# An attention loop where VectorE weighs two value rows, GpSimd two, and TensorE adds the last two sums while it transposes

## What is computed

```
x = x + xattn(layernorm(x), ctx_1024, itok)
x = x + ffn(layernorm(x))

xattn: q = x @ Wq.T ; k, v = split(ctx @ Wkv.T) ; 16 heads of 32
  each row looks at its index and the three before it: 4 keys and 4 values
  probs = softmax(mask(q . k * 32**-0.5))        # over these 4
  out = sum over the 4 of probs * v ; out @ Wo.T
ffn: quantised gate and up (512 to 1536), sigmoid, product, down (1536 to 512)
```

## Time and profile before

| what | us |
|---|---|
| median of 3 runs | 2347.9 |
| the runs | 2347.78 to 2349.55 |
| span of the profiled execution | 2347.3 |

### The profile page before, as it was taken

The page is one execution under the profiler, slowest core; times in us unless marked ns, Lnnn a source line. Parts: engine busy times, 40 slices in busy tenths (PEclk is TensorE's granted clock), DMA queues, the critical chain, the costliest instruction groups (busy, mean ns, idle before and its releaser), DMA issues.

```text
span 2347.3 us, 25386 instructions
## 1 busy us (share of the span) xinstructions
PE 2020.4 (86%) x9524; PEld 945.0 (40%) x9524; DVE 1715.7 (73%) x1387; ACT 1398.2 (60%) x1599; POOL 670.6 (29%) x662
## 2 busy tenths in 40 slices
PE   5888888888599999999999999999000699999998
PEld 2444444444244444444444444444000344444443
DVE  8799999999634534532499998999899644577641
ACT  4678887887422322322499996676899633366530
POOL 2599999998300000000121110222111000000000
PEclk9999999999799999999999999999555899999999
DMA  7789999998346656743699995787998755555541
GB/s 297 283 314 337 348 337 346 335 350 316 126 181 226 225 207 223 259 148 144 242 378 390 378 369 209 264 320 293 401 419 327 291 229 208 205 201 232 233 152 72
DMA packets 131162, 634.60 MB, mean 270 GB/s; under 512 B 12256, under 2 KB 12768, under 8 KB 91104
## 3 DMA queue, kind: packets, MB, share of 16 engines
q1 hardware_dynamic: 85888, 316.81, 37.0%
q0 software_dynamic: 45152, 316.16, 34.6%
HBM read 430.69 MB, written 202.24 MB: 270 GB/s over the span
## 4 chain that ended last, share of the span: by engine, by line
PE 64%; issue 3%; DVE 3%; ACT 2%; POOL 0%; DVEq 0%; ACTq 0%; POOLq 0%
PE fd_pp L1777 42%; PE fd_pp L1791 21%; ACT ff_ring L1720 1%; DVE ff_sig L1575 1%; DVE ff_h_parts L1559 1%; DVE ff_sq L1497 1%; ACT ff_sig L1707 0%; DVE ff_sq L1566 0%; DVE kept_gate L1568 0%; DVE ff_gin L1510 0%; DVE ff_hq L1549 0%; ACT ff_hq L1632 0%; ACT ff_ring L1746 0%; ACT ff_sig L1736 0%; DVE kept_o_peak L1575 0%
## 5 line engine op out<-in xcount | busy, mean ns | idle before, releaser
L1791 PE MATMUL fd_pp<-ff_down,kept_gate 128*128 128x512 f16 x1536 | 458.9, 381 | 193.1 <-DVE ff_up L1616 193.1
L1777 PE MATMUL fd_pp<-ff_h_parts,kept_gate 128*128 128x512 f16 x2304 | 499.6, 380 | 14.3 <-DVE ff_h_parts L1415 14.3
L1777 PE MATMUL fd_pp<-ff_h_parts,ff_up 128*128 128x512 f16 x2304 | 497.4, 379 | 0.0
L1639 ACT ACTIVATE ff_raw<-fd_pp 128x1024 f32<-128x1024 f32 x192 | 194.3, 1017 | 396.5 <-PE fd_pp L1777 396.5
L1777 PEld LDWEIGHTS fd_pp<-ff_h_parts,kept_gate 128*128 128x128 f16 x2304 | 225.9, 98 | 287.9 <-DVE ff_h_parts L1415 14.7
L1777 PEld LDWEIGHTS fd_pp<-ff_h_parts,ff_up 128*128 128x128 f16 x2304 | 225.4, 98 | 271.8
L1420 DVE TENSOR_REDUCE kept_gate_peak<-ff_raw 128x1 f32<-128x2048 f32 x48 | 109.7, 2285 | 292.9 <-ACT ff_raw L1639 292.9
L1791 PEld LDWEIGHTS fd_pp<-ff_down,kept_gate 128*128 128x128 f16 x1536 | 150.6, 98 | 375.9 <-issue 195.8
L1791 PE MATMUL fd_pp<-ff_down,ff_up 128*128 128x512 f16 x768 | 292.2, 380 | 0.0
L1746 ACT ACTIVATE ff_ring<-ff_hq,kept_g 128x2048 int16<-128x2048 f32 x48 | 96.0, 1999 | 191.1 <-DVE ff_hq L1549 189.7
L790 PE MATMUL at_psO<-kept_wo,at_ahi 128*128 128x512 f16 x512 | 155.5, 386 | 36.2 <-ACT at_alo L277 31.6
(11 more groups left out here) (239 smaller groups left out, 3454.9 us busy)
## 6 DMA issues: line engine op xcount, KB each, us to landing
ff_raw<-up_scratch SPq DMA_DIRECT2D x66, 1024.0 KB, 8.5
gate_scratch<-ff_raw POOLq DMA_DIRECT2D x48, 1024.0 KB, 9.1
ff_gin<-gate_scratch SPq DMA_DIRECT2D x48, 1024.0 KB, 8.7
up_scratch<-ff_raw POOLq DMA_DIRECT2D x48, 1024.0 KB, 7.7
ff_gin<-gate_integers SPq DMA_DIRECT2D x73, 512.0 KB, 5.8
gate_integers<-ff_ring POOLq DMA_DIRECT2D x43, 512.0 KB, 8.7
ff_up<-up_scratch SPq DMA_DIRECT2D x21, 1024.0 KB, 9.5
kept_xs<-in_x SPq DMA_DIRECT2D x32, 512.0 KB, 14.6
```

Of the source, the lines that this page charges most:

```text
L1639: nc.scalar.activation(raw[:, n % UNITS, h * 2 * BLK:(h + 1) * 2 * BLK], pp[(2 * n + h) % 4][:, :, :].rearrange("p a t -> p (a t)"), ACT.C ...
L1777: mm = nc.tensor.matmul(pp[k % 4][:, h, :], wt[w][:, c, f:f + P], a[:, b % 2, :, c, :], start=(q == 0), stop=(q == len(todo) - 1))
L1791: mm = nc.tensor.matmul(pp[k % 8 // 2][:, k % 2, :], a[b % 2][:, f, t * P:(t + 1) * P], wt[w][:, f, :], start=(q == 0 and i == 0), stop=(q ...
```

## The change

VectorE weighs value rows 0 and 1 only. GpSimd weighs rows 2 and 3 in one instruction (`weigh_upper`), adds them to rows 0 and 1 as before, and does no second addition. `att` is gone; a tile of the same size that nobody uses keeps the other addresses. TensorE's `turn_a` waits for `half` in place of `att`, transposes row 0 into `psA` as before, and then row 1 into the same bank with four more transposes that add to what is there.

A slot of the ring is now read by TensorE to the end, so the gather into it waits for `aT`. Its place on GpSimd changes too: the gather behind tile 2s-3 stands ahead of the additions of pair `s_`, the one behind 2s-2 stays behind them. In the last pair `sum_last` has only its first addition. SP's two loads for the next section wait for `aT` in place of `att`.

```diff
--- before.py
+++ after.py
@@ -158,7 +158,8 @@
 
         xn = r.sb("xn", [P, 2, D], F32)
         xhi, xlo = (r.sb(n, [P, 2, DC, P], F16) for n in ("xhi", "xlo"))
-        att, hn = (r.sb(n, [P, 2, D], F32) for n in ("att", "hn"))
+        r.sb("gap", [P, 2, D], F32)
+        hn = r.sb("hn", [P, 2, D], F32)
         hT = r.sb("hT", [P, 4, D], F32)
         ahi, alo = (r.sb(n, [P, 2, DC, P], F16) for n in ("ahi", "alo"))
         kv = r.sb("kv_rows", [P, KR, W, 2 * D], F32)
@@ -185,7 +186,7 @@
         x1_out = [r.sem(f"x1_out{i}") for i in range(XR)]
         hT_out = [r.sem(f"hT_out{i}") for i in range(2)]
         rows_in = [r.sem(f"rows_in{i}") for i in range(KR)]
-        m = r.sems("xn xT xhi xrest xlo q prod raw sc top ds ex tot inv pr pv last half att aT ahi arest alo o x1 "
+        m = r.sems("xn xT xhi xrest xlo q prod raw sc top ds ex tot inv pr pv last half aT ahi arest alo o x1 "
                    "nmean ssq ssq_v stat aggr sqe root rstd norm x_nmean x_ssq hn hT hT_sb peak h_red h_all reduced")
 
         def blocks(t, h):
@@ -232,7 +233,7 @@
                         sp.dma_start(x1_v[p], xs[:, ring(p), :]).then_inc(x1_out[p % XR], 16)
                     p = s_ - 5
                     if p == NP - 6:
-                        sp.wait_ge(m["att"], KR * (NT // KR) - KR + 6 if NT % KR == 0 else NT - NT % KR)
+                        sp.wait_ge(m["aT"], NT - NT % KR)
                         for b in range(2):
                             sp.wait_ge(hT_out[0], 16 * (b + 1))
                             sp.wait_ge(hT_out[1], 16 * (b + 1))
@@ -521,8 +522,8 @@
                                             AX.X, ALU.add).then_inc(m["raw"], 1)
 
                 def weigh(t):
-                    values = kv[:, t % KR, 0:W - 1, D:2 * D].rearrange("p w (h e) -> p w h e", h=H)
-                    nc.vector.tensor_tensor(values, values, pr[:, t % 2, 0:W - 1].unsqueeze(3).to_broadcast([P, W - 1, H, HD]),
+                    values = kv[:, t % KR, 0:2, D:2 * D].rearrange("p w (h e) -> p w h e", h=H)
+                    nc.vector.tensor_tensor(values, values, pr[:, t % 2, 0:2].unsqueeze(3).to_broadcast([P, 2, H, HD]),
                                             ALU.mult).then_inc(m["pv"], 1)
 
                 def residual(t):
@@ -542,10 +543,6 @@
                     dve.wait_ge(m["pv"], t + 1)
                     nc.vector.tensor_tensor(kv[:, t % KR, 0:2, D:2 * D], kv[:, t % KR, 0:2, D:2 * D], kv[:, t % KR, 2:4, D:2 * D],
                                             ALU.add).then_inc(m["half"], 1)
-                    dve.wait_ge(m["half"], t + 1)
-                    dve.wait_ge(m["aT"], t - 1)
-                    nc.vector.tensor_tensor(att[:, t % 2, :], kv[:, t % KR, 0, D:2 * D], kv[:, t % KR, 1, D:2 * D],
-                                            ALU.add).then_inc(m["att"], 1)
 
                 def last_moments(t):
                     p, k = t // 2, t - (LAST - 3)
@@ -681,28 +678,25 @@
                                                 in_offset=bass.IndirectOffsetOnAxis(ap=keep["rows"][:, t:t + 1], axis=0),
                                                 element_offset=0).then_inc(rows_in[t % KR], 16)
 
-                def weigh_fourth(t):
-                    last = kv[:, t % KR, W - 1, D:2 * D].rearrange("p (h e) -> p h e", h=H)
+                def weigh_upper(t):
+                    upper = kv[:, t % KR, 2:4, D:2 * D].rearrange("p w (h e) -> p w h e", h=H)
                     pool.wait_ge(rows_in[t % KR], 16 * (t // KR + 1))
                     pool.wait_ge(m["pr"], t // 2 + 1)
                     if t < LAST - 1:
                         pool.wait_ge(m["pv"], t // 2 * 2 + 2)
-                    nc.gpsimd.tensor_tensor(last, last, pr[:, t % 2, W - 1].unsqueeze(2).to_broadcast([P, H, HD]),
+                    nc.gpsimd.tensor_tensor(upper, upper, pr[:, t % 2, 2:4].unsqueeze(3).to_broadcast([P, 2, H, HD]),
                                             ALU.mult).then_inc(m["last"], 1)
 
                 def add_up(t):
-                    weigh_fourth(t)
+                    weigh_upper(t)
                     lower, upper = kv[:, t % KR, 0:2, D:2 * D], kv[:, t % KR, 2:4, D:2 * D]
                     pool.wait_ge(m["last"], t + 1)
                     nc.gpsimd.tensor_tensor(lower, lower, upper, ALU.add).then_inc(m["half"], 1)
-                    pool.wait_ge(m["half"], t + 1)
-                    need(pool, m["aT"], t - 1)
-                    nc.gpsimd.tensor_tensor(att[:, t % 2, :], kv[:, t % KR, 0, D:2 * D], kv[:, t % KR, 1, D:2 * D],
-                                            ALU.add).then_inc(m["att"], 1)
 
                 def gather_next(t):
-                    pool.wait_ge(m["att"], t + 1)
-                    gather(t + KR)
+                    if t + KR < NT:
+                        pool.wait_ge(m["aT"], t + 1)
+                        gather(t + KR)
 
                 for t in range(KR):
                     if t == 0:
@@ -720,13 +714,14 @@
                     gather(t)
                 for s_ in range(NP + 6):
                     if s_ == NP:
-                        weigh_fourth(LAST - 1)
-                        weigh_fourth(LAST)
+                        weigh_upper(LAST - 1)
+                        weigh_upper(LAST)
                     if pair(s_ - 1) and s_ < NP:
+                        if tile(2 * s_ - 3):
+                            gather_next(2 * s_ - 3)
                         add_up(2 * s_ - 2)
                         add_up(2 * s_ - 1)
                         gather_next(2 * s_ - 2)
-                        gather_next(2 * s_ - 1)
                     if s_ > 0 and (pair(s_ - 3) or pair(s_ + 3)):
                         norms(s_)
                 nc.gpsimd.partition_all_reduce(last_all[:, :], eps_d[:, 0:1], P, PEAK).then_inc(m["reduced"], 1)
@@ -818,9 +813,13 @@
                     project(psQ[t % 2], xhi, xlo, wq, t % 2).then_inc(m["q"], 1)
 
                 def turn_a(t):
-                    pe.wait_ge(m["att"], t + 1)
+                    pe.wait_ge(m["half"], t + 1)
                     need(pe, m["alo"], t)
-                    turn(psA, att[:, t % 2, :]).then_inc(m["aT"], 1)
+                    turn(psA, kv[:, t % KR, 0, D:2 * D])
+                    for c in range(DC):
+                        mm = nc.tensor.matmul(psA[:, c, :], kv[:, t % KR, 1, D + c * P:D + (c + 1) * P], ident[:, :], is_transpose=True,
+                                              start=False, stop=(c == DC - 1), skip_group_check=True)
+                    mm.then_inc(m["aT"], 1)
 
                 def rest_a(t):
                     pe.wait_ge(m["ahi"], t + 1)
```

## The result

| | before | after |
|---|---|---|
| median | 2347.84 us | 2375.09 us |
| runs | 2346.82 to 2349.55 (4) | 2374.15 to 2375.44 (4) |
| span of the profiled execution | 2347.3 us | 2373.3 us |

The changed kernel takes 1.0117 times as long, with a 95% interval of 1.0102 to 1.0131. The forecast was 2370.4 us with a range from 2344 to 2380, so it was right in its sign and 4.7 us too low.

The account below looks back on a forecast made before the run. VectorE's back-to-back program was taken to set the 16.95 us pair. 26 pairs at +0.81 (+21.1) and ends of +1.4 gave +22.5 us on the 2347.3 us span, 0.6 under the median: 2370.4 us, range 2344 to 2380.

Parts of the forecast that it names:

- VectorE's and GpSimd's own work: Attention loop, per pair: VectorE's program falls from 16.95 to 15.90 us, GpSimd's tensor work from 9.67 to 8.70 us.
- Rival D: GpSimd's product of 1024 elements costs 2.37 us like an addition: period 17.97 us, 2376 us in all; chance 0.08.
- The wait at the queue's head: GpSimd's odd-tile gather, first in its stage, waits for TensorE's transposes until 1.75 us into each pair; products start at 3.08.
- The eight transposes: TensorE, per tile: eight transposes of `a` take 1.04 us instead of 0.60 for four, 0.44 us more.
- the 6.85 us of the forecast: From the end of VectorE's differences to the end of the odd tile's eight transposes, not shortened by VectorE's shorter weighing.
- The port: VectorE's mask and scale instruction waits for GpSimd's second addition and ends at 11.93 instead of 10.07 us: delay 1.86 us.
- Rival B: Faster: the port costs little; period 15.90 to 16.68 us, middle 16.3, 2331 us in all; chance 0.17.
- Rival C: No change: GpSimd's sequence is some 0.8 us shorter, so the delay eats exactly the weighing's gain; 2349 us; chance 0.09.
- E: Odd gathers land late, each microsecond over 18.0 adding one to a pair; at 19, 2396 us; chance 0.04.
- The period: Steady attention loop: 15.90 + 1.86 = 17.76 us a pair, 0.81 us more than before; bounds 17.4 to 18.2.
- 26 pairs at +0.81: Pairs 5 to 30 of the attention loop, each 0.81 us longer: +21.1 us in the sum.
- The last pair: Longer GpSimd products and transposes 0.9 us longer, against shorter VectorE weighing and no last VectorE addition: +1.4 us.

## Why the prediction was right, and where it was not

**VectorE's and GpSimd's own work.** The two weighings were put at 2.38 us and took 2.36; the product of 1024 at 1.92 us and took 1.920; the additions keep 2.36. Rival D, a product at the price of an addition, fell with this number. The 4.8 us that the prediction read for the norms, as the most that they take, hold some 2.8 us of waiting behind VectorE's weighings; as a bound it did no harm.

**The wait at the queue's head.** Forecast: the wait ends 1.75 us into the pair, the gather runs at 2.03, the products at 3.08 and 7.41, the additions to 11.78. Measured: 2.04, 3.08, 7.40 and 11.75. The eight transposes, put at 0.44 us more than four, have that price by the shorter run without the second four. From the end of `L581` of one pair to the end of the transposes of the next, the 6.85 us of the forecast, it is 6.84 us: 307.30 to 314.14, the end of this row, and the gather starts 0.29 us later.

```profile
313.54 0.60 PE L820 MATMUL at_psA<-kept_ident,at_kv_rows 128*128 128x128 f32 x4
```

**The port.** Forecast: `L571` ends at 11.93; measured 11.90. Rival B, that the port costs little, had a chance of 0.17 and fell in this kernel, but its other half held: with the wait out of the way the pair goes to 16.19 us, under B's bound of 16.68 for the loop of TensorE and ScalarE. It is near B's 16.3, but that was only the middle between 15.90 and 16.68. Rival C would have needed a shorter sequence on GpSimd, and E gathers that land late: `L516` has no idle time ahead of it in pairs 7 to 29.

**The period.** 17.76 us were forecast and 17.72 measured in the normal pairs, 1.0 us less over 25 of them.

**What was missed.** The sum took one period for all pairs. The clock was 1.00 in the earlier trace rows, and I carried that over to a kernel in which TensorE waits longer: six pairs are 0.96 us longer for it, 5.8 us, more than the whole error of the forecast. The step that failed is "26 pairs at +0.81". The mechanism of the sum stands, the term is 21.1 where 26.2 were measured: +5.8 for the clock, +0.25 for pair 5, -1.0 for the normal pairs. What lies outside pairs 5 to 30, forecast at +1.4, came to -0.2, so the span was 3.5 us longer than the sum; the other 1.2 us of the 4.7 lie between span and median, 1.8 us here where 0.6 were taken. Errors of both signs cancel in part, so the total is nearer to the forecast than its terms are.

**The last pair.** Forecast +1.4, measured +0.3. VectorE's first addition of the pair there takes 2.92 us beside GpSimd's second product, and the transposes of tile 62 start 0.37 us later than before, about the 0.5 that the forecast's other terms give. But the transposes, which I made 0.9 us longer, are no longer at all. The windows of these transposes, in the kernel before and in the changed one:

```profile
610.70:611.90 1.20, 1.11 (x4) 0.71 (x4) 1.20 (x2) 0.02 (x1) 0.00 (x0) 0.50 1.01 377
```
```profile
637.60:638.80 1.20, 1.09 (x8) 0.86 (x8) 1.20 (x2) 0.02 (x1) 0.00 (x0) 1.00 1.02 381
```
Four took 1.11 us at a clock of 0.50; eight take 1.09 us at 1.00. I had doubled a row without looking at the clock that it ran at.

## What to carry to other kernels

An instruction that waits at the head of an engine's queue is paid for by all that is queued behind it: before moving one up, look for the time at which its condition is met, and put it behind work that is ready (one place further back was worth 48 us here). The same edit that takes work from the bound engine can make an instruction wait for another engine whose result it does not read; where two engines share a port such a wait is counted as busy time, so look at the length of a small instruction whose work did not change, not at the busy share. And a row taken from a trace belongs to the clock that it ran at: ask of a longer wait on TensorE what it does to the clock.

## What the runs showed of the hardware

- TensorE's granted clock fell to 0.50 for more than 3 us in six of 25 pairs (219.65 to 223.00 in the first), behind two idle stretches of 0.94 and 1.06 us in a stream that was otherwise dense; eight more transposes a pair in the second of them, which left 0.19 us of it, kept it at 1.00.
- An instruction of VectorE that GpSimd holds up is counted as busy all the while, and so is one of GpSimd that VectorE holds up (128x4 elements in 1.63 us beside a weighing, 0.20 without). Released, one of 128x128 elements ends 0.15 us behind GpSimd's instruction, and the addition of 1024 elements in the last pair 1.08 us behind it (608.86 to 609.94 in the kernel before).
- Four transposes in fp32 that add into a PSUM bank take what four plain ones take (273 ns for the last, 0.109 us apart).
- A gather follows a tensor instruction of GpSimd by 0.15 to 0.16 us even where nothing is waited for (300.04 in the run with the gather behind the addition, 324.29 in the changed kernel), which is more than the 0.03 to 0.08 us between its other instructions that depend on each other.
- GpSimd's product with a broadcast operand takes 1.70 ns for each element more (1.048 us at 512 elements in the kernel before, 1.920 at 1024 in the changed one), its addition 2.14 ns (1.275 and 2.370).
